# The key mask of a grouped attention: three matmuls per tile, or an addition on GpSimd an expert layer earlier

## What is computed

```
logits = x @ gate_w.T + gate_b ; keep the top 2
gate_score = softmax(logits)
expert_out = einsum('bsd,edo->bseo', x, expert_w) + expert_b
out = einsum('bseo,bse->bso', expert_out, gate_score)
```

```
Q, K = rope((x @ Wq)), rope((kv @ Wk)) ; V = kv @ Wv
scores = einsum('bhqd,bhkd->bhqk', Q, K) * D ** -0.5
scores = scores + rel_pos_bias[:, rel][None]      # by head, query and key
scores = where(mask[:, None, None, :], scores, -1e9)   # by batch and key
out = softmax(scores) @ V @ Wo
```

## Time and profile before

| | us |
|---|---|
| median of 3 runs (lowest, highest) | 1124.82 (1123.07, 1130.02) |
| the profiled execution | 1123.04 |
| its span | 1121.2 |
| PE busy | 918.0 |
| DVE busy | 721.4 |
| POOL busy | 358.7 |
| granted TensorE clock, mean of the span | 0.918 of full speed |

### The profile page before, as it was taken

The page is one execution under the profiler, slowest core; times in us unless marked ns, Lnnn a source line. Parts: engine busy times, 40 slices in busy tenths (PEclk is TensorE's granted clock), DMA queues, the critical chain, the costliest instruction groups (busy, mean ns, idle before and its releaser), DMA issues. The chain is left out here.

```text
span 1121.2 us, 17317 instructions
## 1 busy us (share of the span) xinstructions
PE 918.0 (82%) x5737; PEld 648.0 (58%) x5737; DVE 721.4 (64%) x1724; ACT 372.3 (33%) x845; POOL 358.7 (32%) x284
## 2 busy tenths in 40 slices
PE   3799887999879985846699289999998608999987
PEld 2677633444467764723487157666676406777767
DVE  6688667666568869869477388888766334243133
ACT  2465530000045556740355033333332301212212
POOL 1567422000056743437155133333332050110111
PEclk9899988999899997968799689999999757999989
DMA  5000099950000008013553720010000374435200
GB/s 163 1 1 0 1 264 272 283 161 0 1 2 1 0 1 240 8 39 107 165 154 118 229 69 33 11 36 17 30 1 1 111 258 145 144 102 175 84 11 18
DMA packets 82473, 96.88 MB, mean 86 GB/s; under 512 B 11778, under 2 KB 75263, under 8 KB 81999
## 3 DMA queue, kind: packets, MB, share of 16 engines
q1 hardware_dynamic: 73577, 80.53, 24.2%
q0 software_dynamic: 5328, 12.70, 3.2%
q10 hardware_dynamic: 3504, 2.84, 0.9%
HBM read 57.94 MB, written 40.07 MB: 87 GB/s over the span
## 5 line engine op out<-in xcount | busy, mean ns | idle before, releaser
L824 PE MATMUL psum<-m_W,lnT 128*128 128x512 f32 x256 | 115.8, 606 | 0.0
L344 POOL TENSOR_TENSOR prob<-prob,a_rden 128x1232 f32<-128x1232 f32 x32 | 71.9, 2248 | 80.5 <-DVE a_rden L416 80.5
L824 PEld LDWEIGHTS psum<-m_W,lnT 128*128 128x128 f32 x256 | 48.0, 192 | 59.9 <-issue 52.7
L2092 PE MATMUL psum<-g_VW,pT 128*128 128x256 f32 (+1 forms) x320 | 75.9, 393 | 1.6 <-ACT pT L2008 1.6
L1845 POOL TENSOR_TENSOR prob<-prob,g_rden 128x1232 f32<-128x1232 f32 x16 | 36.0, 2248 | 126.5 <-DVE g_rden L1945 126.5
L2568 PE MATMUL psum<-x_xT,x_w 128*128 128x320 f32 x256 | 73.5, 447 | 1.5 <-DVE x_xT L2375 1.5
L2092 PEld LDWEIGHTS psum<-g_VW,pT 128*128 128x128 f32 (+1 forms) x320 | 61.3, 196 | 13.5 <-ACT pT L2008 5.3
L2246 POOL DMA_INDIRECT out_x<-x_yt,x_X x20 | 19.7, 985 | 141.7 <-DVE x_yt L2389 141.1
L2568 PEld LDWEIGHTS psum<-x_xT,x_w 128*128 128x128 f32 x256 | 49.9, 196 | 23.5 <-issue 5.0
L771 DVE SCALAR_TENSOR_TENSOR acc<-psum,gates,acc 128x256 f32<-128x256 f32 x96 | 41.8, 478 | 32.7 <-PE psum L824 32.7
L2042 PE MATMUL psum<-g_Wq,lnT 128*128 128x512 f32 x128 | 61.9, 629 | 0.5 <-ACT lnT L1988 0.5
(11 more groups left out here) (443 smaller groups left out, 2024.4 us busy)
## 6 DMA issues: line engine op xcount, KB each, us to landing
routed_rows<-hole SPq DMA_DIRECT2D x8, 2210.0 KB, 24.6
x_w<-in_L_ffn_w SPq DMA_DIRECT2D x16, 512.0 KB, 4.6
x_w<-in_L_ffn_w SPq DMA_DIRECT2D x8, 1024.0 KB, 8.5
m_xb<-routed_rows SPq DMA_DIRECT2D x39, 130.0 KB, 2.1
g_bias<-in_rel_bias SPq DMA_DIRECT2D x8, 616.0 KB, 3.8
expert_rows<-hole SPq DMA_DIRECT2D x1, 4680.0 KB, 30.2
g_VW<-vw_scratch SPq DMA_DIRECT2D x2, 1152.0 KB, 9.0
x_X<-expert_rows SPq DMA_DIRECT2D x8, 260.0 KB, 4.6
```

The source lines that it names most:

```text
L344: nc.gpsimd.tensor_tensor(heads(c.prob[b]), heads(c.prob[b]), rden[b][:, :].unsqueeze(2).to_broadcast([P, H, SK]), ALU.mult).then_inc(norm ...
L824: last = nt.matmul(c.ps[p][:, :], c.lnT[b][:, k * P:(k + 1) * P], W[:, k, p * 512:(p + 1) * 512], start=(k == 0), stop=(k == KC - 1))
L2092: last = nt.matmul(bank_y[:, 0:D], c.pT[b][0:w, j * P:(j + 1) * P], VW[0:w, b, j, :], start=(j == 0), stop=(j == NB - 1))
```

## The change

The mask is added to the position bias once, ahead of time: in `moe0` SP loads the mask row on all partitions (`mraw3`) and the bias tile by tile pair (`rel`), POOL turns the mask into `mrow` and adds it for each of the 16 tiles (`mask_bias`), and SP stores the sums in a DRAM buffer `mb_dram`. `attn_gqa` loads from it, a tile of its own for each t, and has no mask matmuls and no mask setup.

```diff
@@ moe0, SP, behind the fills
+            def load_bias(j):
+                sp.dma_start(rel[j % 2][:, :, :], d["rel_bias"][j * P:(j + 1) * P, :].rearrange("p (h k) -> p h k", k=SK)
+                             ).then_inc(rel_in[j % 2], 16)
+            sp.dma_start(mraw3[:, :], d["mask3"].partition_broadcast(P)).then_inc(row_in, 16)
+            load_bias(0)
+            load_bias(1)
+            for i in range(NT):
+                sp.wait_ge(masked_ok, i + 1)
+                sp.dma_start(c.mb_dram[i * P:(i + 1) * P, :].rearrange("p (h k) -> p h k", k=SK), masked[i % 2][:, :, :]
+                             ).then_inc(masked_out[i % 2], 16)
+                if i % 2 == 1 and i // 2 + 2 < NT // 2:
+                    load_bias(i // 2 + 2)
+            for b in range(2):
+                sp.wait_ge(masked_out[b], 16 * (NT // 2))
@@ moe0, POOL
+            def mask_bias(i):
+
+                pool.wait_ge(rel_in[i // 2 % 2], 16 * (i // 4 + 1))
+                wait(pool, masked_out[i % 2], 16 * (i // 2))
+                nc.gpsimd.tensor_tensor(masked[i % 2][:, :, :], rel[i // 2 % 2][:, :, :],
+                                        mrow[:, i % 2, :].unsqueeze(1).to_broadcast([P, HB, SK]), ALU.add
+                                        ).then_inc(masked_ok, 1)
             pool.wait_ge(s["gT_ok"], 4)
-            pipeline(pool, step, 0, 2, NT, NT)
+            step(0, 0)
+            step(1, 1)
+            pool.wait_ge(row_in, 16)
+            nc.gpsimd.tensor_scalar(mrow[:, :, :].rearrange("p b k -> p (b k)"), mraw3[:, :].bitcast(U8)[:, 0:B * SK], 0.0, NEG,
+                                    ALU.is_equal, ALU.mult).then_inc(row_ok, 1)
+            pool.wait_ge(row_ok, 1)
+            for i in range(2, NT):
+                step(i, i % 2)
+                mask_bias(i - 2)
+            mask_bias(NT - 2)
+            mask_bias(NT - 1)
@@ attn_gqa, SP
-            sp.dma_start(mraw[:, :], d["mask3"]).then_inc(s["kv_in"], 16)
             for j in range(2):
-                sp.dma_start(bias[j][:, :], d["rel_bias"][j * P:(j + 1) * P, :]).then_inc(bias_in[j % 2], 16)
+                sp.dma_start(bias[j][:, :], c.mb_dram[j * P:(j + 1) * P, :]).then_inc(bias_in[j % 2], 16)
...
-            for j in range(2, S // P):
-                sp.wait_ge(s["s_used"], 2 * j - 2)
-                sp.dma_start(bias[j % 2][:, :], d["rel_bias"][j * P:(j + 1) * P, :]).then_inc(bias_in[j % 2], 16)
+            for j in range(2, NT):
+                sp.wait_ge(s["s_used"], j - 1)
+                sp.dma_start(bias[j % 2][:, :], c.mb_dram[j * P:(j + 1) * P, :]).then_inc(bias_in[j % 2], 16)
@@ attn_gqa, DVE
-            dve.wait_ge(s["kv_in"], 16)
-            chain(nv.tensor_scalar(mrow[:, :], mraw[:, :].bitcast(U8)[:, 0:B * SK], 0.0, NEG, ALU.is_equal, ALU.mult))
-            nv.tensor_copy(mtile[:, :, :, :], mrow[:, :].rearrange("a (b k) -> a b k", b=B).unsqueeze(2)
-                           .to_broadcast([1, B, HPB, SK]))
-            nv.memset(ones[:, :], 1.0).then_inc(s["m_ok"], 1)
...
-                dve.wait_ge(bias_in[jb], 16 * (t // 4 + 1) if is_static(t) else t * 4 + (16 - 4 * q))
+                dve.wait_ge(bias_in[b], 16 * (t // 2 + 1))
@@ attn_gqa, PE
-                for q in range(3):
-                    nh = HPB if q < 2 else 4
-                    last = nt.matmul(sview[:, q, 0:nh * SK], ones[:, :],
-                                     mtile[:, b, 0:nh, :].rearrange("a h k -> a (h k)"),
-                                     start=False, stop=True, skip_group_check=True)
...
-            pe.wait_ge(s["m_ok"], 1)
@@ build
+        c.mb_dram = nc.dram_tensor("masked_bias", (NT * P, H * SK), F32, kind="Internal").ap()
```

More of the change, by code:

```diff
@@ L716, in moe0 @@
              "gtile_in", "e_ps", "acc", "bias_ps", "y_used", "x_ok")
+    mraw3, mrow = sb(c, "m0_mraw3", [P, 40], I32), sb(c, "m0_mrow", [P, B, SK])
+    rel = [sb(c, f"m0_rel{j}", [P, HB, SK]) for j in range(2)]
+    masked = [sb(c, f"m0_masked{j}", [P, HB, SK]) for j in range(2)]
+    rel_in = [sem(c, f"m0_rel_in{j}") for j in range(2)]
+    masked_out = [sem(c, f"m0_masked_out{j}") for j in range(2)]
+    row_in, row_ok, masked_ok = sem(c, "m0_row_in"), sem(c, "m0_row_ok"), sem(c, "m0_masked_ok")
     gates = g8(c.gates)
@@ L1798, in attn_gqa @@
     Wq, C, Sn, KB, VW = c.gWq, c.gC, c.gSn, c.gKB, c.gVW
[L1799 to L1802, removed]
     bias = [sb(c, f"g_bias{j}", [P, HB * SK]) for j in range(2)]
@@ L1806, in attn_gqa @@
     rden = [sb(c, f"g_rden{b}", [P, HB]) for b in range(2)]
-    s = sems(c, "g_", *NORM, "kv_in", "m_ok", "q_ps", "roped", "rope_ok", "qT_ps", "qT_ok", "s_ps",
+    s = sems(c, "g_", *NORM, "q_ps", "roped", "rope_ok", "qT_ps", "qT_ok", "s_ps",
              "vw_in", "s_used", "shifted", "exp_ok", "rd_ok", "p_ok", "pT_ps", "pT_ok", "y_ps", "x_ok", "bias0_in", "bias1_in", "links")
@@ L1920, in shift @@
             def shift(t, q):
-                b, jb = q % 2, (q // 2) % 2
+                b = q % 2
                 p = heads(c.prob[b])
                 dve.wait_ge(s["s_ps"], t + 1)
-                dve.wait_ge(bias_in[jb], 16 * (t // 4 + 1) if is_static(t) else t * 4 + (16 - 4 * q))
+                dve.wait_ge(bias_in[b], 16 * (t // 2 + 1))
                 wait(dve, s["pT_ps"], t * 3 - 3)
@@ L1928, in shift @@
                 nv.tensor_tensor(c.prob[b][:, 0:2 * n].rearrange("p (q n) -> p q n", q=2), sview[:, 0:2, 0:n],
-                                 bias[jb][:, 0:2 * n].rearrange("p (q n) -> p q n", q=2), ALU.add)
-                nv.tensor_tensor(c.prob[b][:, 2 * n:HB * SK], sview[:, 2, 0:4 * SK], bias[jb][:, 2 * n:HB * SK],
+                                 bias[b][:, 0:2 * n].rearrange("p (q n) -> p q n", q=2), ALU.add)
+                nv.tensor_tensor(c.prob[b][:, 2 * n:HB * SK], sview[:, 2, 0:4 * SK], bias[b][:, 2 * n:HB * SK],
                                  ALU.add).then_inc(s["s_used"], 1)
@@ L2063, in scores @@
                     o = (m % 3) * 2 * SK
-                    nt.matmul(sview[:, m // 3, o:o + 2 * SK], qT[b][:, m * P:(m + 1) * P],
+                    last = nt.matmul(sview[:, m // 3, o:o + 2 * SK], qT[b][:, m * P:(m + 1) * P],
                               KB[:, b, m // 2, :, :].rearrange("p r k -> p (r k)"),
-                              start=(m % 3 == 0), stop=False, skip_group_check=True)
-                for q in range(3):
-                    nh = HPB if q < 2 else 4
-                    last = nt.matmul(sview[:, q, 0:nh * SK], ones[:, :],
-                                     mtile[:, b, 0:nh, :].rearrange("a h k -> a (h k)"),
-                                     start=False, stop=True, skip_group_check=True)
+                              start=(m % 3 == 0), stop=(m % 3 == 2 or m == HB // 2 - 1), skip_group_check=True)
                 last.then_inc(s["s_ps"], 1)
```

## The result

| | before | changed |
|---|---|---|
| median of the runs (lowest, highest), us | 1127.32 (1123.07, 1130.02), 4 runs | 1176.5 (1174.38, 1179.7), 4 runs |
| span of the profiled execution | 1121.2 | 1174.3 |
| DVE busy | 721.4 | 747.6 |
| POOL busy | 358.7 | 400.2 |

The ratio is 1.0444, 95% interval 1.0418 to 1.0470: slower by 50.1 us (the two medians differ by 49.2). I had said 1168, a loss of 44.5; the time lies inside the range of 1160 to 1178, but near its upper end, 8.5 above the forecast. Of that, 2.5 is the kernel before, whose median over four runs is 1127.32 where the forecast started from 1124.82. The place and the cause are the ones forecast.

The account below looks back on a forecast made before the run. PE was taken as the bound, only just in the grouped attention. A 47.7 pause in the first expert layer plus 2.5 slow start less 5.7 removed made +44.5, so 1168, range 1160 to 1178.

Parts of the forecast that it names:

- The wait and its place: First expert layer: PE stands still 47.7 before tile 2's bias product, as POOL's copy 2 waits behind the mask row's load.
- rival C: Expert layer: DVE's collisions with POOL's additions add up over 13 tiles, 10.5 more, time 1178; chance 0.06.
- The landing, 242.9: `moe0`: the mask row's DMA, queued behind SP's fills and issued no earlier than 228.10, lands at 242.9.
- Slow start, 2.5: `moe0` after the pause: PE's products and bias pair run slowly at first, costing 2.5 (1.7 to 3.0).
- Addition 2.8, mask row 0.7, copy 0.28: POOL's work in `moe0`: with the copy 3.1 per tile, inside 7.69, so POOL keeps up at no cost.
- The layer's end, zero: End of `moe0`: the last addition and store land before DVE ends the layer; zero, up to 2 if stores are slow.
- The removal, 5.7: Attention without mask matmuls and setup: 3.15 late tiles, 1.6 tiles 1 to 8, 0.9 setup; bounds 0 and 11.1.
- The sum: Whole kernel: 47.7 pause plus 2.5 slow start less 5.7 removed, +44.5, giving 1168.
- A: Mask row's DMA is served ahead of the queued fills, landing by 231.9; PE stands 36.7, time 1157; chance 0.06.
- B: Expert layer: stores and loads throttle POOL, copies late, 9.6 per tile, 25 more, time 1192; chance 0.06.
- D: Expert layer: the mask row lands before 196.48, no pause, only the removal is left, 1117 (1119 on the median); chance 0.02.
- E: Forecast with the attention's gain at an end: all of it, 1162, or none, 1173; chance 0.80 together with the forecast.

Follow-up runs that it names:

- x3: Changed kernel with the mask row's load issued ahead of the fills, bias loads left behind them; no time given, `moe0` 4.6 shorter than in the changed kernel.
- x5: Changed kernel with four of the eight `xd2` fills moved from `moe0` to attention 1; span 1142.6, 31.7 below the changed kernel.
- x4: Changed kernel with all nine fills moved from `moe0` to attention 1; 0.9975 of the kernel before.
- x8: x7 with the fills kept on SP in `moe0`, and the mask row, bias loads and stores issued from ACT; 0.9946 of the kernel before.
- x2: Kernel before with the changed `moe0` only, attention still masking by matmuls; 1.0517 of the kernel before.
- x7: x4 with additions 0 and 1 made before copy 2, then one per tile; 0.9947 of the kernel before, median 1120.82 us.
- x1: Kernel before without the mask matmuls and the mask's setup, scores left unmasked; 0.9947 of the kernel before, 6.0 us faster.
- x0: Kernel before, unchanged, profiled once more for its stage lengths; `moe0` 156.3, `middle` 210.2.
- x9: x7 with each addition made twice, a semaphore wait between the two; single time 1122.64, 1.8 above x7's median.

## Why the prediction was right, point by point

- **The wait and its place**: right. One pause, before tile 2's bias product, released by POOL's copy, POOL idle on `mraw3`. x3 moves it by a tile, x5 scales it with the fills, x4 and x8 remove it. That the total lies in the range owes something to luck all the same: it was stretched up to 1178 for rival C, 13 collisions, which did not come, and 1176.5 needs that stretch.
- **The landing, 242.9**: 1.1 too early. From the stage's start I had 101.1; it was 245.3 - 143.07 = 102.2. The last fill took 23.5 to land where I had the 22.4 of the earlier trace rows, and that is nearly all of it. I had not foreseen the 7.82 of the row's own issue, but it ran beside the last fill, and as the row landed 0.2 behind that fill, it can hardly have cost more. The end of the pause came 1.1 late, 48.8 lost for 47.7. In x2, with the same `moe0`, PE starts again 105.0 after the stage's start, 1.5 later than here, so the landing varies by that much.
- **Slow start, 2.5**: 3.3 (11.0 for a tile of 7.69), a little above my upper bound of 3.0, which came from the shorter idle time at the gates.
- **Addition 2.8, mask row 0.7, copy 0.28**: 2.57, 0.76, 0.28. POOL keeps up; 7.69 per tile again (PE's bias products at 257.55 and 265.23).
- **The layer's end, zero**: the step that failed. I looked there for a late store and found none. What was late was PE: three additions back to back held DVE for 5.08 and 2.69, and PE waited 2.69 and then ran slow for 1.7, 4.4 in all. Rival C's mechanism, DVE held by POOL, is real, but the lateness doesn't add up from tile to tile: it is hidden in all other tiles and shows once, where the additions stand together. What I should have priced is not 13 collisions but one pile.
- **The Trainium skill** ("SBUF — State Buffer", Who interferes with whom): I had said that the trace bears the rule out in part. After the change it holds in nearly every tile: DVE's addition of two SBUF operands, 0.43 alone, ends with POOL's addition (2539 ns median, 5.08 for two in a row). Beside POOL's mask operation in the kernel before it does not hold to the end: the 4.54 of the earlier trace rows ended at 171.86, and POOL's operation only at 167.22 + 7.08 = 174.30 (row below). What such a hold costs the rule does not say; in x7 it cost nothing that shows, since DVE had the time.
- **The removal, 5.7**: by time 6.0 (x1). Tiles 1 to 8 gave 1.9 for 1.6, the late tiles 3.9 for 3.15, since their period is 13.15 and not 13.3: from the scores to the transposes it is 862.53 - 860.44 = 2.09; the kernel before has its scores start at 803.20 (below) and its transposes at 806.02, 2.82, so the masks took 0.73 and not 0.63. The start gave something between nothing and 2.7, by the clock, so the 0.9 for the mask's setup is neither confirmed nor refuted. That the sum came so near is thus in part luck: two of its terms were too small, and the third was not measured.

The two rows of the kernel before that these last two points use:
```profile
167.22 7.08 POOL L809 TENSOR_SCALAR maskT<-prob 77x2048 bf16<-77x2048 int32 x1
...
803.20 2.26 PE L2064 MATMUL psum<-g_KB,g_qT 128*128 128x154 f32 x16
```

- **The sum**: `moe0` +50.2 forecast and +56.7 in the profile, which is 1.1 + 0.8 + 4.4 more. By the runs the whole is +50.1 and not +44.5; 6.3 of misses in `moe0` less 0.3 in the removal is 6.0, against the 5.6 between them. By time alone `moe0` lost 58 (x2), 8 above its forecast; the profile of the kernel before had a slow tile 1 (8.80), and in x0, where it took 7.13, `moe0` is 156.3 and not 158.6.
- **Rivals**: A is out, since the row landed behind the fills. B is out, since no copy was late through the stores, even at 7.2 per store (x8). D is out, since the row was never on time in SP's queue. E: the attention gained 6.0 (x1), neither all of 11.1 nor nothing.

## What to carry to other kernels

A small transfer behind bulk ones in the same queue arrived only when these were done, 0.2 behind the last; what an engine needs soon goes ahead of them or onto another engine's queue, or the bulk goes into a stage with room for it. And what stands behind a wait on an in-order engine pays for it: here an 8 x 128 copy that needed nothing of the mask stopped TensorE for 50 us. Additions on GpSimd beside a VectorE with idle time cost nothing that showed here when they stood one to a tile; spread them, and leave none to stand in a row at the end.

## What the runs showed of the hardware that I had not expected

- Whatever came next behind the queued fills held SP in its issue for about 8: the mask row 7.82 and 8.24, a bias load 8.09 (x3). The row took 0.36 ahead of the fills on SP, and 0.36 from ACT's queue beside them. The hold was not added to the landing: the row landed 0.2 behind the last fill.
- Two GpSimd additions with nothing between them held one VectorE addition for 5.08; with a semaphore wait between them (x9) VectorE got in after the first.
- Stages of the same code differ from one execution to the next: `middle` took 205 in three profiles and 210 to 214 in the others, the attention's first part 34.2 to 36.6 and its last step 11.9 or 13.6. The last two go with the granted clock; for `middle` the cause is open. A term of 1 or 2 us read from one profile's stages needs a second profile, or timed runs.
